# Causal self-attention: the two key halves of the exponentials are added on GpSimd before the products with ones

## What is computed

```python
scores = jnp.einsum('bqhd,bkhd->bhqk', Q, Kp) / jnp.sqrt(jnp.float32(HD))
mask = jnp.tril(jnp.ones((Sq, Sk), bool))
scores = jnp.where(mask, scores, -jnp.inf)
a = jax.nn.softmax(scores, axis=-1)
o = jnp.einsum('bhqk,bkhd->bqhd', a, V).reshape(Bq, Sq, Dm)
```

## Time and profile before

| what | value |
|---|---|
| median of three executions | 1019.58 us (1014.75 to 1019.98) |
| the profiled execution | 1020.12 us, span 1018.2 us |
| busy in the span | TensorE 864.7 us, VectorE 735.1 us, ScalarE 627.7 us, GpSimd 552.2 us |
| mean granted clock of TensorE | 0.917 of 2.4 GHz |
| SA's products with the exponentials | 587.0 us to 740.3 us of the span |

### The profile page before, as it was taken

How to read it: one execution, slowest core, us unless ns; L and a number is a source line. 1 busy time by engine, 2 the same in 40 slices (tenths; PEclk the granted TensorE clock), 3 DMA queues, 4 the chain that set the end, 5 groups by cost and what they waited for, 6 DMA issues and landing times.

```text
span 1018.2 us, 23625 instructions
## 1 busy us (share of the span) xinstructions
PE 864.7 (85%) x8576; PEld 528.5 (52%) x8576; DVE 735.1 (72%) x1592; ACT 627.7 (62%) x1551; POOL 552.2 (54%) x1069
## 2 busy tenths in 40 slices
PE   5888888865556779998998899998998879998996
PEld 2344444433334445555755455565555457675675
DVE  4788888778774655666556767677467587999876
ACT  0899999959883214553355356654555467685775
POOL 2588888866652335663345556656244244555523
PEclk9799999875557889999999899999999789999998
DMA  8500000000000000000000000000000000000000
GB/s 254 174 2 2 0 0 2 2 1 0 1 1 1 0 1 1 2 2 1 1 2 2 24 25 24 23 23 17 1 2 3 1 1 2 2 7 6 10 4 22
DMA packets 23579, 16.48 MB, mean 16 GB/s; under 512 B 8744, under 2 KB 20400, under 8 KB 23344
## 3 DMA queue, kind: packets, MB, share of 16 engines
q1 hardware_dynamic: 23472, 15.06, 5.2%
HBM read 10.85 MB, written 1.05 MB: 12 GB/s over the span
## 4 chain that ended last, share of the span: by engine, by line
PE 51%; DVE 20%; POOL 13%; issue 8%; ACT 6%; SPq 1%; DMA 1%; POOLq 0%; DVEq 0%; ACTq 0%
POOL sb_E L2314 10%; PE ps_context L796 5%; PE ps_context L799 3%; PE ps_scores L872 3%; ACT sb_E L1264 3%; DVE sb_inv_den L1804 2%; PE ps_scores L896 2%; PE ps_turned L1164 2%; PE ps_scores L749 2%; PE ps_scores L789 2%; PE ps_turned L1166 2%; PE ps_turned L1165 2%; PE ps_turned L1102 2%; DVE sb_neg_half L1772 2%; PE ps_scores L1143 2%
## 5 line engine op out<-in xcount | busy, mean ns | idle before, releaser
L1264 ACT ACTIVATE sb_E<-ps_scores,sb_neg_max,sb_score_scale 128x256 f32<-128x256 f32 (+1 forms) x384 | 191.0, 513 | 20.5 <-DVE sb_neg_max L1565 14.5
L2314 POOL TENSOR_SCALAR sb_E<-sb_E,sb_inv_sum 128x256 f16<-128x256 f32 x256 | 124.4, 486 | 26.7 <-DVE sb_inv_sum L1601 7.2
L1517 ACT ACTIVATE sb_E<-ps_scores,sb_ff_bias 128x512 f32<-128x512 f32 x128 | 88.2, 691 | 53.9 <-PE ps_scores L1143 50.4
L1772 DVE TENSOR_REDUCE sb_neg_half<-ps_scores 128x16 f32<-128x1024 f32 x48 | 58.6, 1222 | 67.1 <-PE ps_scores L872 67.1
L1584 DVE TENSOR_REDUCE sb_neg_quad<-ps_scores 128x2 f32<-128x512 f32 (+1 forms) x96 | 64.4, 684 | 41.7 <-PE ps_scores L751 29.7
L1292 ACT ACTIVATE sb_E<-ps_scores 128x512 f32<-128x512 f32 x96 | 57.0, 598 | 48.0 <-PE ps_scores L791 46.8
L1389 ACT ACTIVATE sb_E<-ps_scores 128x1024 f32<-128x1024 f32 x48 | 49.2, 1024 | 55.4 <-PE ps_scores L904 55.4
L710 PE MATMUL ps_turned<-sb_ident 128*128 128x512 f16 x262 | 74.8, 405 | 9.8 <-DVE sb_ident_b L2181 9.8
L1560 DVE TENSOR_REDUCE sb_neg_raw<-ps_scores 128x4 f32<-128x1024 f32 x64 | 77.6, 1212 | 4.6 <-PE ps_scores L682 4.4
L1264 ACT ACTIVATION_READ_ACCUMULATOR sb_E<-ps_scores,sb_neg_max,sb_score_scale 128x1 f32 x384 | 78.5, 205 | 0.0
L2249 POOL TENSOR_SCALAR sb_veps<-sb_mv 128x2 f32<-128x2 f32 x72 | 18.4, 256 | 107.0 <-DVE sb_mv L1542 102.8
(11 more groups left out here) (302 smaller groups left out, 2577.8 us busy)
## 6 DMA issues: line engine op xcount, KB each, us to landing
sb_moe_up<-in_moe_up SPq DMA_DIRECT2D x1, 2048.0 KB
sb_KS<-sb_qk_parts SPq DMA_DIRECT2D x96, 16.0 KB, 1.8
sb_QS<-sb_qk_parts SPq DMA_DIRECT2D x96, 16.0 KB, 1.8
sb_rows<-in_rows SPq DMA_DIRECT2D x1, 1216.0 KB, 8.0
out_x<-sb_raw_context SPq DMA_DIRECT2D x8, 128.0 KB, 1.8
sb_X<-in_x SPq DMA_DIRECT2D x1, 768.0 KB, 10.6
sb_square<-in_square SPq DMA_DIRECT2D x1, 768.0 KB, 11.1
sb_ctxT<-in_ctxT SPq DMA_DIRECT2D x1, 512.0 KB, 11.3
```

Source lines behind the costliest of these rows:

```text
L1264: last = act.activation(E[:, ring, head], SC[t % 2][:, head], ACT.Exp, bias=neg_max[:, ring, h:h + 1], scale=scale, accum_out=row_sum[:, r ...
L1517: last = act.activation(U_full[:, n % RING, :], banks[n % 4], ACT.Gelu, bias=bias, scale=1 / WEIGHT_SCALE)
L1772: dve.tensor_reduce(neg_half[:, n % 2, :, :, :].rearrange("p x i g -> p (x i g)"), SC[0][:, :].rearrange("p (h k) -> p h k", k=CTX), AX.X, ...
L2314: last = pool.tensor_scalar(E16[:, ring, SEQ * h:SEQ * h + SEQ], E[:, ring, SEQ * h:SEQ * h + SEQ], inv_sum[:, ring, h:h + 1], HALF, ALU.m ...
```

## The change

In values, the products with V32 stay as they are. The products with quad_ones change: values(n, 0) reads only the columns of the earlier 128 queries, and values(n, 1) reads, in place of the later keys' exponentials, U[:, n % 2, :], which holds for the later 128 queries the sum of both key halves. GpSimd makes that sum in add_halves, one tensor_tensor of 128 x 512 float32 a unit, as the first thing of its SA step n for unit n - 3. It waits for all exponentials of the unit and for the products of the unit two before (the last readers of that half of U). TensorE waits for the sum in values(n, 1), between the products with V32 and those with quad_ones.

```diff
@@ counts
-                 max_turned=n, max_landed=n, valued=n, keyed=n, keyed_v=n)
+                 max_turned=n, max_landed=n, valued=n, keyed=n, keyed_v=n, added_halves=n)
@@ values (TensorE)
-                if kt == 0:
-                    products(lambda g: V32[:, b, 0, 4 * g + u, :], quad_ones[:, u, :],
-                             lambda g: src[:, SEQ * g:SEQ * g + SEQ], 0, SEQ, u == 0, False)
-                    return
-                last = products(lambda g: V32[:, b, 1, 4 * g + u, :], quad_ones[:, u, :],
-                                lambda g: src[:, UNIT + P * g:UNIT + P * g + P], P, P, False, u == 3)
-                last.then_inc(S["valued"], 1)
+                at, width = (0, SEQ) if kt == 0 else (P, P)
+                for g in range(4):
+                    c = SEQ * g if kt == 0 else UNIT + P * g
+                    pe.matmul(CO[32 * g:32 * g + 32, at:at + width], V32[:, b, kt, 4 * g + u, :], src[:, c:c + width],
+                              start=(u == 0 and kt == 0), stop=(u == 3 and kt == 1), skip_group_check=True)
+                if kt == 1:
+                    pe.wait_ge(S["added_halves"], B["added_halves"] + n + 1)
+                for g in range(4):
+                    both = src[:, SEQ * g:SEQ * g + P] if kt == 0 else U[:, n % 2, P * g:P * g + P]
+                    last = pe.matmul(CO[32 * g:32 * g + 32, SEQ + at:SEQ + at + P], quad_ones[:, u, :], both, start=False,
+                                     stop=(u == 3), skip_group_check=True)
+                if kt == 1:
+                    last.then_inc(S["valued"], 1)
@@ GpSimd
+            def add_halves(L, B, n):
+
+                if not live(n, L.UNITS):
+                    return
+                pool.wait_ge(S["exped"], B["exped"] + L.banks * (n + 1))
+                wait(pool, S["valued"], B["valued"] + n - 1)
+                first = PT[:, n % 2, 0:UNIT].rearrange("p (g q) -> p g q", g=QUADS)[:, :, P:SEQ]
+                second = PT[:, n % 2, UNIT:UNIT + 4 * P].rearrange("p (g q) -> p g q", g=QUADS)
+                pool.tensor_tensor(U[:, n % 2, :].rearrange("p (g q) -> p g q", g=QUADS), first, second, ALU.add)\
+                    .then_inc(S["added_halves"], 1)
+
             def self_step(L, B, n):
                 b, t = n // QUADS, n % QUADS
+                add_halves(L, B, n - 3)
                 quad_keys(L, B, n + 2)
                 if t == 2:
                     cross_base(L, B, b + 2)
```

## The result

The changed kernel took 1027.65 us in the median of 7 runs (1020.94 to 1029.24), the kernel before 1019.58 in 7 beside it: the ratio is 1.0072 with an interval of 1.0042 to 1.0103. So it is slower, and by the ratio itself by more than 0.5% (the low end of the interval is a little under that), the side that was given a chance of 0.22: by 7.3 us after the ratio and 8.1 after the two medians, where the sum said 1.6. The range of the forecast, 1014.5 to 1028, holds the 1027.65 with 0.35 us to spare. The profiled execution took 1028.31 us (span 1026.5), 8.2 more than the one before.

What follows compares the result with a forecast made beforehand. The prediction took TensorE to bound SA; a 7.0 us saving against stalls of 4.6, 1.2 and 2.8 us gave +1.6 us, 1021.2 on the median or 1021.7 on the profiled execution, stated as 1021.5, range 1014.5 to 1028 us.

Steps and rivals of the forecast that it cites:

- the sum: Whole kernel: TensorE's saving of 7.0 us against stalls of 4.6, 1.2 and 2.8 us, together +1.6 us.
- The forecast as worked out: Whole kernel: stalls at their places and the addition at 1.14 to 1.51 us; 1019 to 1024.5 us, chance 0.62.
- the rival of the clock: Behind TensorE's new stalls: waits lower its clock, 1.7 us lost per drop; 1023 to 1033 us, chance 0.13.
- the stall in step 34: End of SA: TensorE waits for the sum because GpSimd has CA's step 1 in front of it; 2.8 us.
- The last mark: From 740 us to the last layer's start: a length change above 1 us would make the prediction wrong.
- The addition on GpSimd: One float32 addition of 128 x 512 per unit on GpSimd: 1.22 us, with ends of 1.14 and 1.51.
- Five stalls in steps with t = 0: Steps 8, 12, 16, 20 and 24: TensorE waits for GpSimd's late sum, 0.92 us each, 4.6 us together.
- Step 31: End of SA: TensorE waits for the sum because GpSimd has CA's step -2 in front; 1.2 us.
- A batch: Four steps in the middle of SA: 18.50 us less 0.85 saved plus a 0.92 us stall, 18.6 us.
- hidden, everywhere: Throughout SA: additions cause no stalls; 1013 us, chance 0.07 if wholly so, 1017 us, chance 0.08 if in part.
- dearer than its neighbours: GpSimd's additions in SA: each takes more than 1.51 us; 1025 to 1031 us, chance 0.10.
- None of it is hidden: TensorE's shortened products in SA: the full 7.0 us saving counts, even where TensorE waits for VectorE in steps 27 to 32.

Runs made afterwards that it cites:

- e7: Changed kernel plus 12 TensorE products of zeros by 512 columns in front of the wait of step 34; 1020.13 us, ratio 1.0011 to the kernel before.
- e2: Kernel before with the change made for the last unit (31) alone; 1031.31 us, ratio 1.0118 to the kernel before.
- e6: Changed kernel's shortened products without additions or waits, later queries' denominators wrong, for timing only; 1011.73 us, ratio 0.9946 to the kernel before.
- e4: Changed kernel with only unit 31's addition moved in front of CA's step 1; 1021.0 us, ratio 1.0020 to the kernel before.
- e5: Changed kernel's additions on GpSimd, but TensorE keeps the old products and doesn't wait for them; 1018.88 us, ratio 0.9999 to the kernel before.
- e3: Changed kernel with every addition a step earlier on GpSimd, behind split_halves of the step before; 1015.71 us, ratio 0.9953 to the kernel before.
- e1: Changed kernel with the last unit (31) keeping its old products and getting no addition; 1017.8 us, ratio 0.9982 to the kernel before.

## Where the prediction held, and where it was wrong

That the range held the time is luck, and no credit to the sum behind it. What lay between 1024.5 and 1028 was put there for several drops of the clock or for a dear addition, and neither came. The forecast as worked out, up to 1024.5 and with a chance of 0.62, didn't come either. What came is the rival of the clock, which had 0.13, but with one long drop where it had reckoned with several short ones.

**The step that failed** is the size of a rival, "The waits bring the clock down". It said of the stall in step 34: "If it has the same effect, some 3.5 us of work run at half speed, 1.7 us are lost: 1022.9. It decides for slower only if the stalls of 0.9 us do the same too". The place was right, and so was the cause. The size was taken from the only drop in the rows shown of before, 0.84 in the mean over 11 us, and used as if each drop were as long. The drop behind step 34 lasted about 27 us. What it costs can be read at the three starts: the kernel after is level at 727.9, then 5.0, then 11.8 us behind. Of this 2.2 is the wait and 9.5 the clock, by the comparison with e7 above. e2 measures the whole by itself, 12.0 us, and e7 takes the clock's part away. So one stall could decide for slower, where I had asked for several.

The forecast had what it needed to be wary: in that stretch everything hangs on TensorE's next scores ("Nothing takes it back"), and the row had one drop, of which nothing told what ends it. One example gives no upper bound, and I took one from it. A longer one stood in the same trace, outside the rows shown. Behind a wait of 1.30 us TensorE ran at half the clock from 797.7 to 808.0, some 10 us, which cost 4.0 us (21.39 instead of 17.35 in the comparison above). Timeline of TensorE, before, and the granted clock in a stretch of it:

```profile
796.67 0.68 PE L958 MATMUL ps_turned<-sb_square,sb_context 128*128 128x128 f32 x4 [1.30 <-DVE sb_context L1806]
...
802.90 1.08 PE L799 MATMUL ps_context<-sb_E,sb_pair_ones 128*32 128x256 f32 x8
```

```profile
800.00:805.00 5.00, 3.86 (x31) 2.00 (x26) 1.94 (x2) 1.02 (x1) 0.00 (x0) 0.50 0.00 0
```

The rival also said of the short stalls that "what a wait of 0.9 us does no row here shows". One did: the wait of 0.86 us lies in the row from 703 to 729, which is at 1.00.

The last mark that the prediction had set itself, "if the stretch from 740 to the start of the last layer changes its length by more than 1 us", is the one that came in.

**What was right.** Point by point, with predicted values first:

- The addition on GpSimd: 1.22 (1.14 to 1.51), measured 1.27 us in the mean of 31 of the 32:

```profile
L2309 POOL TENSOR_TENSOR sb_U<-sb_E 128x512 f32<-128x512 f32 x31 | 39.5, 1273 | 0.3
```

- Five stalls in steps with t = 0, each 0.92 with its restart: 0.68 to 0.89 of waiting, and 0.42 us of the chain for the group behind, instead of 0.22. In e6, without stalls, the like batch takes 17.65 us (643.39 to 661.04, starts of the value projection), 0.89 less than with one. No stall in steps with t = 1 to 3 before step 31, nor in 4 and 28.
- Step 31: 1.2, measured 0.93 of waiting. Step 34: 2.8 with its restart, measured 2.48 of waiting; from the group in front to the group behind it is 2.88 us instead of the 0.21 of e4 (744.43 to 744.64), so 2.67.
- A batch: 18.6, measured 18.54. The rival "hidden, everywhere" is out by that and by the seven waits; "dearer than its neighbours" by the 1.27 us and by e5.

**A smaller error: "None of it is hidden".** Some 0.2 us were, in step 27. VectorE makes four multiplications for CA's keys there, and the maxima of the next scores come behind them; TensorE waits for those (0.43 us before). With shorter products it gets there earlier and waits longer (0.64 in e6, 0.72 in the changed kernel). That row before, after and in e3:

```profile
701.17 0.39 PE L749 MATMUL ps_scores<-sb_KBD,sb_QS 96*128 96x512 f16 x1 [0.43 <-DVE sb_neg_quad L1584]
```

```profile
701.12 0.39 PE L749 MATMUL ps_scores<-sb_KBD,sb_QS 96*128 96x512 f16 x1 [0.72 <-DVE sb_neg_quad L1590]
```

```profile
703.80 0.39 PE L749 MATMUL ps_scores<-sb_KBD,sb_QS 96*128 96x512 f16 x1 [1.32 <-DVE sb_neg_quad L1590]
```

I had argued that VectorE's own start there depends on the shortened group. It does for the maxima, but not for the four multiplications, which stand in front of them. In the stretch up to step 32 the sum's terms make 29 x 0.213 = 6.2 us less 5.8 us of stalls, a gain of 0.4, and it came out level (136.65 against 136.64); the 0.3 us of longer waiting in step 27 are most of the difference. So the terms of the sum were right in that stretch, each on its own and not only by cancelling: e6, without its drop, would save 6.0 us there, and the changed kernel takes 6.0 us more than that.

**What stays open.** What makes one drop last 3.4 us, another 10 and another 27 is not settled. The length of the wait doesn't decide it alone. The wait of 2.16 us in front of the transposition was followed by a drop of about 3.4 us in seven of the nine traces, by one of 6.8 in e6 and by none in e3; the wait of 1.8 us in front of the value projection of step 28 by none in eight, and by one in e6; one of 1.30 us by 10 us at half clock. The wait of 2.48 us stands in two traces (e2 and after), and the long drop is in both and in no other. In both this wait begins some 3 us after a short drop had ended, and no run has it without that one, so whether the wait of 2.48 us would do it alone is not shown. The drop behind the wait of 2.16 us at 732 ended near 736.6. The long one began at 743.3, and TensorE was busy all the way through it. The Trainium skill (TensorE: Matmul & The Clock Gate, Part 1) has sustained work release the clock again; here the row from 742 to 770 shows 27.83 busy us of 28 at 0.53, so continuous work of this kind did not for 27 us. Nor is it shown that every execution of the changed kernel has the long drop. Its fastest of seven, 1020.94, has the highest mean granted clock of them (0.923, where the slowest, 1029.24, has 0.908). It may have gone without, and that would explain why the median lost 7.3 to 8.1 us and not 12. Short drops that cost 1.6 us each are in several traces (19.54 instead of 17.96 us on the ruler in e1 and e5, 17.94 instead of 16.37 us in the next stretch of the changed kernel and e3), and they move from one kernel to another; they may well be much of the spread of a few us around these medians.

## What to carry to other kernels

A wait put into an engine that bounds the kernel is not priced by its length alone: one of 2.5 us took 12 us here, since TensorE's clock fell behind it for ten times as long, while six of 0.7 to 0.9 us took little more than they lasted. So price the longest wait by itself, and look for drops of the clock in the whole trace and not only in the rows of one stage. Where such a wait can't be moved, try to fill it with matmuls that compute nothing. And before adding work to an engine with room, place it by its queue: the same 32 additions made the kernel 0.7% slower in front of GpSimd's step and 0.5% faster behind the split of the step before, where they fill its own waits.

## What the runs showed of the hardware beside that

VectorE's multiplications are slower beside GpSimd's additions; in e5 the additions are the only new work on either engine. The multiplication of float16 keys by picks, 128 x 256, from 590 to 700 us (VectorE's groups by line and shape; total, then mean in ns), before, after and with the additions alone (e5):

```profile
L1713 DVE TENSOR_SCALAR sb_KBD<-sb_KS,sb_picks 128x256 f16<-128x256 f16 x23 | 6.5, 281 | 0.0
```

```profile
L1719 DVE TENSOR_SCALAR sb_KBD<-sb_KS,sb_picks 128x256 f16<-128x256 f16 x23 | 8.1, 351 | 0.0
```

```profile
L1731 DVE TENSOR_SCALAR sb_KBD<-sb_KS,sb_picks 128x256 f16<-128x256 f16 x24 | 9.5, 395 | 0.0
```

Its maxima out of PSUM don't change. In e3 one addition falls on the four multiplications of step 27, and they take 3.45 us instead of 2.90; that is 0.55 of the 0.60 us by which the wait of step 27 is longer than in the changed kernel. The timelines of VectorE and GpSimd, before and in e3:

```profile
697.61 2.90 DVE L1744 TENSOR_SCALAR sb_E<-sb_qk_parts,sb_picks 128x512 f16<-128x512 f16 x4
...
697.58 2.80 POOL L2340 TENSOR_SCALAR sb_E<-sb_qk_parts,sb_picks 128x512 f16<-128x512 f16 x4
```

```profile
699.69 3.45 DVE L1750 TENSOR_SCALAR sb_E<-sb_qk_parts,sb_picks 128x512 f16<-128x512 f16 x4
...
699.63 1.26 POOL L2309 TENSOR_TENSOR sb_U<-sb_E 128x512 f32<-128x512 f32 x1
```

Before, both engines multiply float16 at the same time for 2.8 us and VectorE takes 2.90; beside 1.26 us of a float32 addition of two inputs it takes 0.55 more. The Trainium skill (SBUF — State Buffer, SBUF: two separate sides) describes a pair of ports that VectorE in its faster modes and GpSimd take in turn, the later one blocked for the whole instruction. The slower multiplications agree with it in direction only: VectorE's four began 0.06 us after the addition and took 0.55 us longer, under half of its 1.26. The pair of like multiplications at 697.6, 2.90 and 2.80 us side by side, shows no such blocking.
